# A deformable convolution followed by attention: gathered samples scaled and combined two tiles ahead of TensorE instead of one

## The reference

```
# layer 0: deformable 3x3 convolution on the group-normalised image
offset = conv3x3(gn(x), offset_w) + offset_b           # 18 numbers a pixel
p      = pixel position + tap position + offset
x_off  = g_lt * x[q_lt] + g_rb * x[q_rb] + g_lb * x[q_lb] + g_rt * x[q_rt]   # 9 taps
x      = x + conv(x_off, conv_w)
# layer 1, on tokens (a pixel is a token of 128 numbers)
t = t + causal_attention(ln(t), Wq, Wk, Wv)             # one head, 3136 tokens an image
t = t + experts(ln(t), gate, weight1, weight2)          # 64 experts, 8 tokens an expert and image
```

## Time and profile before

| | |
|---|---|
| median of 3 runs | 2898.94 us (2898.17 to 2901.55) |
| span of the profiled execution, first to last instruction | 2895.9 us |
| TensorE matmuls / weight loads busy | 2702.8 us / 2123.3 us |
| VectorE / ScalarE busy | 1887.0 us / 1785.9 us |
| GpSimd busy (1800 gathers) | 1758.3 us |
| mean granted TensorE clock | 0.977 |

### The profile page before, as it was taken

One profiled execution on the slowest core, in us unless ns is written; L12 is line 12 of the kernel. 1 busy time (PEld: TensorE's weight loads), 2 busy tenths in 40 slices (PEclk: granted clock), 3 DMA queues, 4 the chain that ended last, 5 costly groups with the idle time before them and its releaser, 6 DMA issues. The chain is left out here.

```text
span 2895.9 us, 53454 instructions
## 1 busy us (share of the span) xinstructions
PE 2702.8 (93%) x19102; PEld 2123.3 (73%) x19102; DVE 1887.0 (65%) x7235; ACT 1785.9 (62%) x4118; POOL 1758.3 (61%) x1831
## 2 busy tenths in 40 slices
PE   5688999999999999999999999999999998899787
PEld 3466787778777887778777787778777787777664
DVE  3466675767577775866677775866677766765425
ACT  3455666666675666666676666666676666665430
POOL 5777775776577755776577755776577756750000
PEclk8899999999999999999999999999999999999889
DMA  6455334633255324633255323643255323432199
GB/s 187 119 148 139 112 114 120 169 110 103 86 158 140 109 86 118 164 117 98 88 156 141 113 84 118 155 124 97 85 158 152 116 84 95 126 82 95 28 397 394
DMA packets 218212, 382.59 MB, mean 132 GB/s; under 512 B 43849, under 2 KB 128777, under 8 KB 217051
## 3 DMA queue, kind: packets, MB, share of 16 engines
q0 software_dynamic: 88992, 250.76, 30.0%
q1 hardware_dynamic: 126363, 113.95, 13.1%
q10 hardware_dynamic: 2592, 14.45, 1.2%
HBM read 316.90 MB, written 62.13 MB: 131 GB/s over the span
## 5 line engine op out<-in xcount | busy, mean ns | idle before, releaser
L532 POOL DMA_INDIRECT shared<-pair_table,idx x1800 | 1737.8, 965 | 836.4 <-issue 527.7
L1144 PEld LDWEIGHTS bank_o<-vals,prob_t 128*128 128x128 f32 x5200 | 634.4, 192 | 130.3 <-ACT prob_t L579 65.3
L1144 PE MATMUL bank_o<-vals,prob_t 128*128 128x128 f32 x5200 | 663.2, 277 | 31.5 <-ACT prob_t L579 31.5
L579 ACT ACTIVATE prob_t<-bank_r 128x512 f32<-128x512 f32 (+3 forms) x728 | 383.3, 548 | 479.8 <-PE bank_r L1131 479.0
L834 DVE CUSTOM_DVE_ANT_0 prob<-bank_r,mask 128x512 f32<-128x512 f32 (+3 forms) x728 | 449.9, 628 | 310.4 <-PE bank_r L1122 308.0
L1122 PE MATMUL bank_r<-keys,qt 128*128 128x512 f32 (+3 forms) x1456 | 640.7, 556 | 0.0
L824 DVE SCALAR_TENSOR_TENSOR shared<-shared,wb 128x128 f32<-128x128 f32 x1800 | 516.6, 347 | 160.4 <-ACT shared L560 159.7
L560 ACT ACTIVATE shared<-shared,wa 128x128 f32<-128x128 f32 x1800 | 561.6, 392 | 42.7 <-DMA shared<-pair_table,idx 42.6
L1111 PEld LDWEIGHTS bank_r<-convw_t,smp_t 128*128 128x128 f32 x3600 | 444.2, 194 | 56.8 <-issue 36.3
L1111 PE MATMUL bank_r<-convw_t,smp_t 128*128 128x128 f32 x3600 | 477.5, 279 | 1.5 <-ACT smp_t L565 1.5
L1131 PE MATMUL bank_r<-ident,prob 128*128 128x128 f32 x2600 | 382.2, 274 | 13.8 <-ACT prob L657 13.8
(11 more groups left out here) (168 smaller groups left out, 2235.7 us busy)
## 6 DMA issues: line engine op xcount, KB each, us to landing
shared<-in_dram SPq DMA_DIRECT2D x32, 1024.0 KB, 17.9
shared<-pair_table,idx POOLq DMA_INDIRECT x1800
pair_table<-rows_out SPq DMA_DIRECT2D x112, 256.0 KB
t<-in_dram SPq DMA_DIRECT2D x48, 256.0 KB, 3.9
t_dram<-t SPq DMA_DIRECT2D x48, 256.0 KB
shared<-in_dram SPq DMA_DIRECT2D x7, 1568.0 KB
stage<-t_dram POOLq DMA_DIRECT2D x8, 832.0 KB, 7.5
pm_dram<-logit SPq DMA_DIRECT2D x8, 800.0 KB
```

The costliest lines, as they stand in the source:

```text
L532: pool.indirect_dma_start(g[t % RING][:, n, :], None, pair_table[b % 2], bass.IndirectOffsetOnAxis(ap=idx[:, b % 2, i * TAPS + n:i * TAPS ...
L579: act.activation(prob_t[q % 3][:, 0:w], ring_bank(("prob", t, c))[:, 0:w], ACT.Copy)\
L1144: last = pe.matmul(attn_ps, prob_t[q % 3][:, n * P:(n + 1) * P], vals[:, slot(tb, at), :], start=(at == 0), stop=(at == ti))
```

## The change

A constant AHEAD = 2 takes the place of the 1 in `step + 1`, for scaling on ScalarE and for the sums on VectorE. Before the loop both engines do tiles 0 and 1 instead of tile 0. GpSimd, TensorE, SyncE, the buffers and the ring of banks are the same.

```
+AHEAD = 2
 ...
-            for p in range(PIECES):
-                scale_first(0, p)
+            for t in range(AHEAD):
+                for p in range(PIECES):
+                    scale_first(t, p)
 ...
-                pieces = list(range(PIECES)) if step + 1 < ALL else []
+                pieces = list(range(PIECES)) if step + AHEAD < ALL else []
                 while pieces and not early:
-                    scale_first(step + 1, pieces.pop(0))
+                    scale_first(step + AHEAD, pieces.pop(0))
 ...
                     if early and pieces:
-                        scale_first(step + 1, pieces.pop(0))
+                        scale_first(step + AHEAD, pieces.pop(0))
 ...
                 for p in pieces:
-                    scale_first(step + 1, p)
+                    scale_first(step + AHEAD, p)
 ...
-            for p in range(PIECES):
-                add_second(0, p)
+            for t in range(AHEAD):
+                for p in range(PIECES):
+                    add_second(t, p)
 ...
-                pieces = list(range(PIECES)) if step + 1 < ALL else []
+                pieces = list(range(PIECES)) if step + AHEAD < ALL else []
 ...
                     if chunks_in(v) >= 4 and c >= 2 and pieces:
-                        add_second(step + 1, pieces.pop(0))
+                        add_second(step + AHEAD, pieces.pop(0))
 ...
                 for p in pieces:
-                    add_second(step + 1, p)
+                    add_second(step + AHEAD, p)
```

## The result

| | before | changed |
|---|---|---|
| median | 2898.85 us (4 runs, 2898.17 to 2901.55) | 2845.7 us (4 runs, 2844.67 to 2847.78) |
| ratio | | 0.9815, 95% interval 0.980 to 0.983 |
| span of the profiled execution | 2895.9 us | 2843.9 us (that execution: 2845.91) |

The change gains 53 us; the spans differ by 52.0. Forecast were 52.2 and 2847 us.

What follows compares the result with a forecast made beforehand. GpSimd's gathers bound image 0 until about tile 16; afterwards TensorE's waits in steps 16 to 22 remained. Gains of 48.2 + 3 + 1 = 52.2 us off the 2895.9 us span, plus 3.0, gave 2847 us; range 2830 to 2886.

Steps and rivals of the forecast that it cites:

- stage two: Images 1 to 7: gathers are long done when scaled; remaining waits are 7.4 us an image, all in steps 16 to 22.
- stage one: Image 0: GpSimd's gathers, nine per 11.1 us, are the bound until about tile 16.
- The wait of L1103: Transposes waiting for VectorE's sums: the wait goes whole, gaining 7.4 us in images 1 to 5, 5.6 in 6 and 7; 48.2 us.
- its wait, but at most what L1111 has in hand: Each step's gain is capped by the products' slack after the sample eviction: 3.2 us in step 18, 0.87 in step 22.
- The clock: Step 18's half-clock dips in images 1 to 5, 1.8 us each, vanish with the waits; image 0's half-clock stretches grow.
- Image 7 from step 7 to 15: At 2438 to 2490 us, 9.2 us of waits; between 0 and 9.2, a gain of 3 us was taken.
- Image 0: Products run one gather later through the gather-bound part, later repaid; net about 1 us gained, ends 11 lost and 8 gained.
- A: The wait moves: TensorE finds evictions, Exp or score banks not ready; each step gains about half; 2872 us, chance 0.24.
- C: Slower: ScalarE's order paces the kernel; image 0's blocked scaling costs 11 us throughout, nothing returns elsewhere; 2910 us, chance 0.08.
- B: All 72.5 us of waits outside image 0's gather-bound part go, with the dips; 2817 us at most, chance 0.07.
- D: No effect: gathers or banks keep TensorE from coming earlier and image 0 comes out even; 2899 us, chance 0.06.

Runs made afterwards that it cites:

- only_16_22: Two tiles ahead only for tiles 16 to 22 of images 1 to 7, one ahead for all others; 2845.4 us, ratio 0.9818 to the kernel before.
- hybrid: One tile ahead up to tile 22, two from tile 23 on, where the changed kernel has two throughout; 2842.72 us, ratio 0.9809 to the kernel before.
- image0_only: Two tiles ahead only in tiles 0 to 24, then one ahead as in the kernel before; 2900.21 us, ratio 1.0004 to that kernel.
- copies_first: The changed kernel with ScalarE's three copies of transposed samples ahead of Exp in every step; 2840.16 us, ratio 0.9796 to the kernel before.
- ahead_3: The changed kernel with three tiles ahead instead of two; 2868.49 us, ratio 0.9895 to the kernel before.

## Why the prediction was right, point by point

*What bounds the kernel.* Right on both stages. `only_16_22` shows stage two with its seven steps and `hybrid` stage one.

*The wait of L1103.* The terms, per image, forecast and measured. An image's gain is split by the length from one tile's first product to the next, which changed from tile 15 on as 11.4 to 10.0, 11.4 to 10.2, 13.7 to 10.5, 10.7 to 9.5, then 13.3 to 12.5 (tile 21) and 12.0 to 11.6:

| step | forecast | measured |
|---|---|---|
| 16 | 1.5 | 1.4 |
| 17 | 1.1 | 1.2 |
| 18, with a clock dip (images 1 to 5) | 3.0 | 3.2 |
| 18, without (images 6, 7) | 1.2 | 1.5 |
| 19 | 1.0 | 1.2 |
| 20 | 0.2 | 0.1 |
| 22 | 0.6 | 1.2 (0.8, and 0.4 after it) |
| sum, images 1, 4 and 5 | 7.4 | 8.3 (8.6 with the rest of the image) |

The rule of "its wait, but at most what L1111 has in hand" was right for step 18. Where there was no dip it does better than the forecast of 1.2, which was got by taking the dip off 3.0: the rule itself, on rows of image 6 in the kernel before, gives the 1.5 that was measured. The wait there is 2.2 us as in image 1, the first copy is out about 2234.42, and L1111 follows 1.5 us later:

```profile
2233.93 1.22 ACT L565 ACTIVATE smp_t<-bank_r 128x384 f32<-128x384 f32 x3
...
2235.96 0.19 PEld L1111 LDWEIGHTS bank_r<-convw_t,smp_t 128*128 128x128 f32 x1 [0.24 <-issue]
```

For step 22 it was too strict by 0.6 us: the first product gained 0.8, and the other 0.4 came back before the next tile, since only the first piece was short. The timeline there, with the earlier trace rows beside it:

```profile
641.93 1.23 ACT L566 ACTIVATE smp_t<-bank_r 128x384 f32<-128x384 f32 x3
642.45 1.19 PEld L1114 LDWEIGHTS bank_r<-convw_t,smp_t 128*128 128x128 f32 x10 [0.69 <-ACT smp_t L566]
```

Over images 1 to 5 the sum was 39.9 us (2.3 + 37.6) for 37.0, and would have been 43 but for two new half-clock stretches, in step 12 or 13 of images 2 and 3:

```profile
846.00:869.00 23.00, 20.97 (x152) 17.52 (x150) 16.79 (x66) 14.71 (x39) 17.82 (x18) 0.93 0.74 148
1171.50:1180.50 9.00, 7.91 (x48) 5.96 (x47) 6.78 (x25) 5.87 (x16) 7.17 (x7) 0.81 0.58 153
```

`hybrid` has clock 1.00 in the same steps and is 1.6 us quicker in each of the two. Images 6 and 7 (from tile 190 on) gave 7.0 and 6.6 for 5.6 each.

*The clock.* That the dip of step 18 goes was right; that the waits make it was not the whole of it. In the changed kernel the step runs at full clock in all images:

```profile
912.60:922.80 10.20, 10.08 (x74) 8.30 (x73) 8.56 (x32) 8.31 (x23) 7.86 (x8) 1.00 0.34 102
1233.30:1243.50 10.20, 10.08 (x74) 8.29 (x73) 8.59 (x32) 8.31 (x23) 7.76 (x9) 1.00 0.37 107
```

But `image0_only` has the same three waits without the dip in images 1 and 5 and with it in images 2 to 4. In image 1 its order is that of the kernel before, and the step begins 1.3 us later; so the waits are not enough for a dip, and what in the place of the step decides is not shown. The Trainium skill's rule ("TensorE: Matmul & The Clock Gate", Part 1), idle time bringing the half clock back, fits the steps looked at, which all have waits ahead of the dip; but in step 12 of image 2 `hybrid` waits the same 2.0 us for its probabilities as the changed kernel, without the dip. The other forecast made by it came true: the granted clock of image 0 fell.

```profile
60.00:241.00 181.00, 137.52 (x863) 104.79 (x864) 99.45 (x391) 94.57 (x253) 137.32 (x144) 0.87 0.50 142
60.00:241.00 181.00, 129.03 (x807) 103.00 (x808) 98.03 (x380) 90.64 (x250) 137.43 (x144) 0.80 0.46 134
```

The first line is the kernel before, the second the changed one.

*Image 7 from step 7 to 15.* A term that was mis-sized: 3 us forecast, 0.5 measured (-44.6 to -45.1). What stands there now, in the stretch that was 2438 to 2490 us before:

```profile
PEld bank_o L1147 <- ACT prob_t L580: 6.5, 3, 3.4
PEld bank_r L1035 <- DVE vals L900: 3.4, 2, 2.9
```

```profile
2393.00:2445.00 52.00, 42.11 (x271) 35.31 (x270) 45.35 (x175) 37.18 (x104) 40.43 (x39) 0.90 0.38 113
```

Both waits were there before, with 5.7 and 1.1 us, so they took back 3.1 of the 9.2 us. About 3 us more went to the clock, 0.90 for 0.97: the changed kernel has about 10 us of half clock here, the kernel before 3. Two stretches are new. One, in step 12, makes that step 13.1 us long for 11.4 in `hybrid`, which has clock 1.00 there; one in step 8 costs 1.3 us, as the same step without and with it in the kernel before (9.1 us) and in `image0_only` (10.4) tells. Without them the steps would have gained about 3.5 us, an estimate from these four lengths; some 2.5 us are not traced. So the forecast of 3 was fair for the waits, and what it lacked was that half-clock stretches would come in here.

*Image 0.* Forecast 1 us of gain, measured 2.3 of loss, inside the ends of -8 and +11. The failed figure is "it moves to about 234, and hits gather 17, which then lands near 246": step 15 was 13.4 us late and not 8. The 8 us came from "about 11 us less what the old sequence spent from scaling to products", and this was wrong: nothing comes off. Tile 15's product stood 10.6 us behind the start of a scaling before, of its own tile, and again 10.6 us behind one after, of tile 16. Before:

```profile
219.38 2.73 ACT L560 ACTIVATE shared<-shared,wa 128x128 f32<-128x128 f32 x9 [1.39 <-DMA shared<-pair_table,idx]
...
229.99 1.19 PEld L1111 LDWEIGHTS bank_r<-convw_t,smp_t 128*128 128x128 f32 x10 [0.81 <-issue]
```

Changed:

```profile
232.76 2.73 ACT L561 ACTIVATE shared<-shared,wa 128x128 f32<-128x128 f32 x9 [1.89 <-DMA shared<-pair_table,idx]
...
243.34 1.42 PEld L1114 LDWEIGHTS bank_r<-convw_t,smp_t 128*128 128x128 f32 x12 [0.81 <-issue]
```

So the delay is the whole gather period of 11.3 us. Most of the other 2 us is that the gathers themselves did not come "at the old times": the first was issued at 36.58 for 35.50, and the last of tile 16 ended 1.5 us later. Why is not shown. With the late step 15 the load went out at 239.78, and gather 17 was scaled from 251.35:

```profile
251.35 2.74 ACT L561 ACTIVATE shared<-shared,wa 128x128 f32<-128x128 f32 x9 [4.05 <-DMA shared<-pair_table,idx]
...
256.34 0.97 PEld L1114 LDWEIGHTS bank_r<-convw_t,smp_t 128*128 128x128 f32 x8 [1.53 <-ACT smp_t L566]
```

The products of step 16 came at 256.3 for 252, 9.2 us late. Of these 6.9 were repaid up to tile 25, as the waits in steps 17 to 22 and the gap to the gathers allowed (5.9 forecast).

*The rivals.* A: the wait at the copies did come, 72.4 us in all and 33.6 of it in image 0, but `copies_first` prices it at half a microsecond an image. C: its first half is real, and `ahead_3` shows that once the waits of steps 16 to 22 are spent nothing repays it; its second half failed with the result itself, in which every later image gained 6.9 us or more. B and D fell with the sum.

The total was nearer than its terms deserve, and that is luck: -3.3 us in image 0 and -2.5 in image 7 offset about +5 in the steps of stage two.

## What to carry to other kernels

When an in-order engine prepares work for another, price a step of more distance in two sums: the waits that it removes, each capped by what the next consumer has in hand, and in every stretch in which the source (here a gather) is no further ahead than the new distance, one period of the source, with all that is queued behind the blocked instruction. Where the two stretches are apart, let the distance differ: here one tile until the gathers have a lead, two from then on. Place the change of distance in a step whose doubled work stands ahead of nothing urgent, and keep large transfers out of the stretch without lead.

## What the runs showed of the hardware

- A 1568 KB load from DRAM issued while indirect gathers run delayed the landing of the gather in flight to 9.7 us after its issue had ended, where about 2 us was usual. Moved to s = 20 it cost ScalarE a wait of 8.38 us there; at s = 22 it cost 6.2 us in one profiled execution and none in those of two other kernels.
- Identical orders with identical waits had a half-clock stretch (1.2 GHz) of TensorE in one image and none in the next; a stretch costs 1.3 to 1.8 us here, and kernels that differ by 1 us in an early step have them in different places. Two such stretches are 3 us of a whole run, so for smaller effects the starts of single tiles tell more than medians.
